# A recurrence of 1024 steps with its side work behind each step: one reciprocal, attention's product and the injections of gi, f and o each placed at another step

## The reference, cut to what matters

```python
x = x + L0(x, cond)   # attention over two keys (a learned one and one from cond), 16 heads, projected
x = x + L1(x, cond)   # mixture of experts: a shared one (silu gate) and the best 2 of 8, weighed
x = x + L2(cond, x)   # u @ W_u + x @ W_e, u from cond
x = x + L3(x, cond)   # LSTM over the 1024 positions, h0 = cond, c0 = 0

# L1: s = sigmoid(x @ router + t_bias); top 2 of s + bias; gates = s_sel / (sum(s_sel) + EPS)
#     out = (shared + sum over the two of gate * expert(x)) / 3
# L3: z = x_t @ Wx + b + h @ Wh; i, f, o = sigmoid; g = tanh; c = f * c + i * g; h = o * tanh(c)
```

## Time and profile before

| | us |
|---|---|
| median of 3 runs | 2413.18 (2410.02 to 2414.47) |
| the profiled execution: time | 2409.16 |
| its span, first to last instruction | 2407.4 |
| TensorE busy (matmul) | 2051.9 (85%) |
| VectorE busy | 1420.3 (59%) |
| POOL busy | 1169.1 (49%) |
| ScalarE busy | 876.7 (36%) |

### The profile page before, as it was taken

One profiled execution on the slowest core, in us unless ns is written; L12 is line 12 of the kernel. 1 busy time (PEld: TensorE's weight loads), 2 busy tenths in 40 slices (PEclk: granted clock), 3 DMA queues, 4 the chain that ended last, 5 costly groups with the idle time before them and its releaser, 6 DMA issues.

```text
span 2407.4 us, 200920 instructions
## 1 busy us (share of the span) xinstructions
PE 2051.9 (85%) x86306; PEld 1505.9 (63%) x86306; DVE 1420.3 (59%) x7602; ACT 876.7 (36%) x4761; POOL 1169.1 (49%) x5082
## 2 busy tenths in 40 slices
PE   6888888888888888888888888888888888888888
PEld 4666666666666666666666666666666666666666
DVE  2565665566566556656655665665566566556655
ACT  1333333333333333333333333333333333333333
POOL 3445445444544554454455445445544544544454
PEclk8999999999999999999999999999999999999999
DMA  3000000000000000000000000000000000000000
GB/s 135 4 3 2 3 3 2 2 3 3 2 3 3 2 2 3 3 2 3 3 2 2 3 3 2 3 3 2 2 3 3 2 3 3 2 2 3 3 2 3
DMA packets 57581, 14.54 MB, mean 6 GB/s; under 512 B 56161, under 2 KB 56161, under 8 KB 57058
## 3 DMA queue, kind: packets, MB, share of 16 engines
q1 hardware_dynamic: 57570, 14.39, 2.6%
HBM read 12.26 MB, written 2.10 MB: 6 GB/s over the span
## 4 chain that ended last, share of the span: by engine, by line
PE 37%; POOL 22%; DVE 20%; issue 12%; ACT 9%; DVEq 0%; POOLq 0%; ACTq 0%
PE bank L885 28%; DVE bank L678 9%; ACT terms L513 5%; DVE bank L686 5%; PE bank L792 5%; DVE h_ring L702 4%; ACT bank L519 4%; PE bank L742 3%; POOL beats L386 2%; POOL ties L387 2%; POOL ties L389 2%; POOL beats L391 2%; POOL lead L384 2%; POOL beats L358 1%; POOL top L394 1%
## 5 line engine op out<-in xcount | busy, mean ns | idle before, releaser
L885 PEld LDWEIGHTS bank<-wh_sb,h_ring 128*4 128x4 f32 (+2 forms) x65536 | 922.9, 94 | 705.9 <-DVE h_ring L702 700.1
L885 PE MATMUL bank<-wh_sb,h_ring 128*4 128x64 f32 (+2 forms) x65536 | 1107.9, 219 | 296.8 <-DVE h_ring L702 229.7
L510 ACT ACTIVATE f_act<-bank 128x4 f32<-128x4 f32 x1024 | 177.3, 173 | 1026.0 <-DVE bank L676 1026.0
L676 DVE STREAM_TRANSPOSE bank<-bank 128x64 f32<-128x64 f32 x1024 | 271.6, 265 | 390.7 <-PE bank L885 390.7
L678 DVE STREAM_TRANSPOSE bank<-bank 128x64 f32<-128x64 f32 x1024 | 271.5, 265 | 186.1 <-PE bank L885 186.1
L513 ACT ACTIVATE terms<-bank 128x8 f32<-128x8 f32 x1024 | 189.5, 185 | 280.3 <-DVE bank L678 280.3
L372 POOL TENSOR_TENSOR num<-one,fall 128x8 f32<-128x8 f32 x130 | 26.0, 200 | 532.1 <-ACT fall L467 532.1
L754 PE MATMUL bank<-up_sb,x 128*32 128x512 f32 x2080 | 274.0, 599 | 0.7 <-ACT fall L467 0.7
L684 DVE STREAM_TRANSPOSE bank<-bank 128x64 f32<-128x64 f32 x1024 | 271.6, 265 | 0.1
L760 PE MATMUL bank<-down_e,hid_t 128*16 128x256 f32 x3096 | 266.6, 380 | 0.0
L702 DVE SCALAR_TENSOR_TENSOR h_ring<-o_act,bank 128x4 f32<-128x4 f32 x1024 | 161.0, 157 | 138.6 <-ACT bank L519 95.0
(11 more groups left out here) (133 smaller groups left out, 2654.2 us busy)
## 6 DMA issues: line engine op xcount, KB each, us to landing
x_a<-in_x SPq DMA_DIRECT2D x129, 16.0 KB, 1.7
x_s<-in_x SPq DMA_DIRECT2D x129, 16.0 KB, 1.7
up_sb<-in_up SPq DMA_DIRECT2D x1, 2048.0 KB, 8.7
out_y<-y_sb SPq DMA_DIRECT2D x128, 16.0 KB, 1.4
down_sb<-in_down SPq DMA_DIRECT2D x1, 1536.0 KB, 12.5
wx_sb<-in_wx SPq DMA_DIRECT2D x1, 1024.0 KB, 14.2
wh_sb<-in_wh SPq DMA_DIRECT2D x1, 1024.0 KB, 16.3
wkv_sb<-in_wkv SPq DMA_DIRECT2D x1, 512.0 KB, 3.9
```

Source lines behind the costliest of these rows:

```text
L510: nc.scalar.activation(f_act[:, :].rearrange("p (c b) -> p c b", b=B), t_f_b[:, :, fo:fo + B], ACT.Tanh).then_inc(a_f, 1)
L676: nc.vector.transpose(bank[3][:, 0:HC], z_f_b[:, 0:HC]).then_inc(t_f, 1)
L885: last = nc.tensor.matmul(z[32 * j:32 * j + row + B, 0:HC], h_ring[:, prev, c, WIN - B - row:WIN], wh_v[:, c, g, j, :], start=False, stop= ...
```

## The change

- VectorE: `invert_inv` goes from step 5 (between scan and L702) to step 7, behind `hidden_s` and in front of the first transpose. The transpose of `hid_s` goes from the front of step 0 to step 7, between scan and L702.
- TensorE: `attend` goes from step 7 to step 3, behind `sum_mm`, and its product from bank 5 to bank 7; `x3_made` is signalled behind it. gi is injected behind step 6 (`GI_AT`), f and o behind step 7. `stream_made`, for which `attended` waits, is signalled behind `down_mm(0)` and not behind the two products of the stream.
- ScalarE and `recur`: the offsets of the rows change places between gi and f, o.
- POOL: `pad` goes from behind `gates` into it, between `lead` and `beats`, and copies other columns of x3.
- In front of the loop: a third product of attention stands behind x3, and the transpose of hid_s for the first batch of the loop is made there.

```diff
-FO_AT = 6
+GI_AT = 6
...
-        attn_b = bank[5][:, 64:64 + C * NB].rearrange("p (c t) -> p c t", c=C)
         partial_b = bank[7][:, 0:D]
         x3_b = bank[7][:, D:D + C * NB].rearrange("p (c t) -> p c t", c=C)
+        attn_b = bank[7][:, D + C * NB:D + 2 * C * NB].rearrange("p (c t) -> p c t", c=C)
+        attn_first_b = bank[6][:, C * NB:2 * C * NB].rearrange("p (c t) -> p c t", c=C)
...
+            BEHIND = (GI_AT + 1) * B
+
             def pad(count):
                 pool.wait_ge(x3_out, count)
-                return pool.tensor_copy(padded[:, :, NB:2 * NB], x3[:, :, NB:2 * NB])
+                return pool.tensor_copy(padded[:, :, NB:2 * NB], x3[:, :, BEHIND:BEHIND + NB])
...
                 pool.tensor_tensor(lead[:, :, :], rivals, own_sel, ALU.subtract).then_inc(gate_step, 1)
+                if between:
+                    between()
                 pool.wait_ge(gate_step, 7)
...
-                gates(i * U + (READY + U))
-                pad(i * U + (READY + U)).then_inc(padded_out, U)
+                gates(i * U + (READY + U), lambda: pad(i * U + (READY + U)).then_inc(padded_out, U))
                 weigh(i * U + (READY + U)).then_inc(hid_e_out, U)
...
-                    if u == 0:
-                        dve.wait_ge(hid_s_out, now)
-                        turn(0, hid_s[:, :], hid_st, U)
-                    elif u == 1:
+                    if u == 1:
...
                     elif u == 7:
-                        hidden_s(now, U)
+                        hidden_s(now)
+                        invert_inv(now)
                     dve.wait_ge(z_f, now)
...
-                    elif u == 5:
-                        invert_inv(now)
                     elif u == 6:
                         hidden_a(now)
+                    elif u == 7:
+                        dve.wait_ge(hid_s_out, now)
+                        turn(0, hid_s[:, :], hid_st, U)
...
-            pe.wait_ge(own_first, 3)
-            pe.wait_ge(hid_s_out, 3 * U)
-            attend()
...
-            sum_mm(READY)
+            sum_mm().then_inc(x3_made, READY)
+            pe.wait_ge(own_first, 3)
+            pe.wait_ge(x3_out, READY)
+            attend(attn_b)
...
-                    fo = (u + U - FO_AT - 1) % U * B
+                    gi = (u + U - GI_AT - 1) % U * B
                     now = pe.snap(t + (u + 1))
                     pe.wait_ge(hid, now)
-                    recur(z_f_b, GF, fo, prev).then_inc(z_f, 1)
-                    recur(z_gi_b, GC, u * B, prev)
-                    recur(z_gi_b, GI, 16 + u * B, prev).then_inc(z_gi, 1)
-                    recur(z_o_b, GO, fo, prev).then_inc(z_o, 1)
+                    recur(z_f_b, GF, u * B, prev).then_inc(z_f, 1)
+                    recur(z_gi_b, GC, gi, prev)
+                    recur(z_gi_b, GI, 16 + gi, prev).then_inc(z_gi, 1)
+                    recur(z_o_b, GO, u * B, prev).then_inc(z_o, 1)
                     if u == 0:
 
                         pe.wait_ge(hid_st, now)
-                        stream_mm(U)
+                        stream_mm()
                         cond_mm()
-                        down_mm(0)
+                        down_mm(0).then_inc(stream_made, U)
...
                     elif u == 3:
                         pe.wait_ge(partial_out, now)
-                        sum_mm(U)
+                        sum_mm()
+                        pe.wait_ge(own_out, now)
+
+                        attend(attn_b).then_inc(x3_made, U)
...
                     elif u == 6:
+                        pe.wait_ge(padded_out, now)
+                        pe.wait_ge(t_gi, now)
+                        inject_gi()
+                    elif u == 7:
                         pe.wait_ge(t_f, now)
                         inject_fo(z_f_b, GF)
                         pe.wait_ge(t_o, now)
                         inject_fo(z_o_b, GO)
-                    elif u == 7:
-                        pe.wait_ge(padded_out, now)
-                        pe.wait_ge(t_gi, now)
-                        inject_gi()
-                        pe.wait_ge(own_out, now)
-                        attend()
```

More of the change, by code:

```diff
@@ L362, in add_eight, with gates @@
                 pool.tensor_tensor(out, terms[:, :, 0:1], terms[:, :, 1:2], ALU.add).then_inc(gate_step, 1)
-            def gates(count):
+            def gates(count, between=None):
                 rivals = sel[:, :].unsqueeze(1).to_broadcast([P, E, E])
@@ L585, in invert_inv, with attended @@
                 nc.vector.reciprocal(inv[:, :], den_eps[:, :]).then_inc(inv_out, U)
-            def attended(src):
-                nc.vector.tensor_tensor(x1[:, :, :, 0:NB], attn_b.unsqueeze(2).to_broadcast([P, C, J, NB]),
+            def attended(attn, src):
+                nc.vector.tensor_tensor(x1[:, :, :, 0:NB], attn.unsqueeze(2).to_broadcast([P, C, J, NB]),
                                         src.unsqueeze(2).to_broadcast([P, C, J, NB]), ALU.add).then_inc(x1_out, U)
@@ L594, in hidden_a, with hidden_s @@
                                                op0=ALU.add, op1=ALU.mult).then_inc(hid_a_out, U)
-            def hidden_s(count, up_to):
+            def hidden_s(count):
                 dve.wait_ge(hid_a_out, count)
-                nc.vector.tensor_tensor(hid_s[:, :], hid_a[:, :], units[:, P:2 * P], ALU.mult).then_inc(hid_s_out, up_to)
+                nc.vector.tensor_tensor(hid_s[:, :], hid_a[:, :], units[:, P:2 * P], ALU.mult).then_inc(hid_s_out, U)
             def turn(unit, src, done, up_to):
@@ L615, in _ @@
             dve.wait_ge(attn_made, 1)
-            attended(x_first[:, 0, :, :])
+            attended(attn_first_b, x_first[:, 0, :, :])
             mask_first(1)
@@ L621, in _ @@
             hidden_a(U)
-            hidden_s(U, U)
+            hidden_s(U)
             dve.wait_ge(hid_s_out, U)
@@ L632, in _ @@
             dve.wait_ge(attn_made, 2)
-            attended(x_first[:, 1, :, :])
+            attended(attn_first_b, x_first[:, 1, :, :])
             mask_first(2)
@@ L643, in _ @@
             hidden_a(2 * U)
-            hidden_s(2 * U, 2 * U)
+            hidden_s(2 * U)
             dve.wait_ge(x3_made, READY)
             layer3(READY)
+            dve.wait_ge(hid_s_out, 2 * U)
+            turn(0, hid_s[:, :], hid_st, U)
             dve.wait_ge(w_in["wh"], 16)
@@ L738, in scores, with attend @@
                     nc.tensor.matmul(scores_b, score_w[:, c, :], x_s[:, c, :], start=(c == 0), stop=(c == C - 1))
-            def attend():
+            def attend(attn):
                 for c in range(C):
-                    last = nc.tensor.matmul(attn_b[:, c, :], value_w[:, c * P:(c + 1) * P], w1_own[:, :],
+                    last = nc.tensor.matmul(attn[:, c, :], value_w[:, c * P:(c + 1) * P], w1_own[:, :],
                                             start=True, stop=True)
@@ L761, in tile_mm, with stream_mm @@
                                         skip_group_check=True)
-            def stream_mm(up_to):
+            def stream_mm():
                 for c in range(C):
                     last = tile_mm(c, x1[:, c, 0, 0:NB], we_sb[:, c, :], True)
-                last.then_inc(stream_made, up_to)
+                return last
             def cond_mm():
@@ L776, in down_mm, with sum_mm @@
                 return last
-            def sum_mm(up_to):
+            def sum_mm():
                 for c in range(C):
@@ L781, in sum_mm @@
                                             start=True, stop=True)
-                last.then_inc(x3_made, up_to)
+                return last
             wh_v = wh_sb[:, :, :].rearrange("p c (g j m) -> p c g j m", g=4, j=J)
@@ L795, in inject @@
                 return last
-            BEHIND = (FO_AT + 1) * B
             def inject_fo(z, g):
-                return inject(z, g, NB, x3[:, :, BEHIND:BEHIND + NB], ones[:, 16:32], True)
+                return inject(z, g, NB, x3[:, :, NB:2 * NB], ones[:, 16:32], True)
             def inject_gi():
@@ L821, in _ @@
             pe.wait_ge(own_first, 1)
-            attend().then_inc(attn_made, 1)
+            attend(attn_first_b).then_inc(attn_made, 1)
             pe.wait_ge(value_out, 3)
@@ L831, in _ @@
             pe.wait_ge(we_ident, C)
-            stream_mm(READY)
+            stream_mm().then_inc(stream_made, READY)
             pe.wait_ge(w_in["wproj2"], 16)
@@ L839, in _ @@
             pe.wait_ge(own_first, 2)
+            attend(attn_first_b).then_inc(attn_made, 1)
+            pe.wait_ge(x1_out, 2 * U)
             pe.wait_ge(hid_s_out, U)
-            attend().then_inc(attn_made, 1)
-            pe.wait_ge(x1_out, 2 * U)
             route()
```

11 lines of the change are left out of this document (5 added, 6 removed).

## The result

The changed kernel takes 2218.28 us (median of 4 runs, 2215.42 to 2219.01) against 2412.98 (the median of 4 as well; the 2413.18 above is that of 3): ratio 0.9192, 95% interval 0.9176 to 0.9208. The forecast was 2209 in a range of 2201 to 2247. The direction, the two places and the range hold; 9 us of the forecast gain did not come, and 2218.28 lies 1.3 over the stretch of 2201 to 2217 that the prediction gave 0.70.

What follows compares the result with a forecast made beforehand. The prediction took one ring's latency across engines as the bound, with side work delaying steps 5 and 7. It summed 129.3 + 76.2 - 1 = 204.5 us off, giving 2204.7, plus 4.0 to the median: about 2209, range 2201 to 2247.

Steps and rivals of the forecast that it cites:

- the two places: Step 5, where L702 is 1.03 us late behind the reciprocal, and step 7, where TensorE is 0.60 late.
- gi's overrun: Rival: gi's injection overruns step 6, 17 us more, 2226; chance 0.10.
- the prediction's own sign: The prediction is wrong if a step other than 0 is over 2.1; that step names the failed part.
- part 4: POOL's pad moves between lead and beats; beats and all behind come 0.3 us later, the waiting reciprocal having 1.1 slack.
- The reciprocal, 129 us: VectorE's last reciprocal leaves step 5, and the wait holding L702 goes: 1.01 x 128 = 129.3 us gained.
- Step 7 from 2.68 to 2.08: TensorE's step 7 swaps gi's injection and attention's product for the injections of f and o: 76.2 us gained.
- The bound from above: TensorE's jump at the end of step 7, taken from VectorE's 0.45: 0.16 us late, 20 us over 127 batches.
- the jump shows: Rival: TensorE's jump to the loop's head, with 0.29 us of cover, adds 20 us: 2229; chance 0.12.
- gi's injection in step 6 costs nothing: TensorE's injection of gi in step 6 ends at 1.98, before 2.08; cost taken as 0, at most 17 us.
- POOL and h_read: half_h ends by 1213.85, before L702 of step 0 at 1214.7, 0.85 spare; rival POOL bound, 2292, chance 0.04.
- The transpose in step 7, and step 0 as before: VectorE's transpose of hid_s, moved between scan and L702 in step 7, costs nothing; step 0 keeps its 2.14.
- Slower by instruction fetch: Rival: each jump at the loop's head costs the first entry's 2.28 us gap, giving 2461; chance 0.02.

Runs made afterwards that it cites:

- e2: Kernel before, with the last reciprocal moved to step 7 and pad between lead and beats, TensorE's order unchanged: 2286.8 us, ratio 0.9481.
- e1: Kernel before, with only the last reciprocal moved from step 5 to step 7 behind hidden_s: 2420.88 us, ratio 1.0040.
- e5: e4 with the injections back where they were, f and o behind step 6, gi behind step 7: 2226.1 us, ratio 0.9237.
- e4: Changed kernel, with pad on POOL later, behind the three additions of s_sum and in front of den_eps: 2206.79 us, ratio 0.9152.
- e6: Changed kernel, with one more unused 128x8 addition on POOL between pad and beats: 2207.16 us, ratio 0.9160.
- e7: e4 with VectorE's step 0 wait for h_read moved earlier, in front of the wait for a_f: 2196.95 us, ratio 0.9120.
- e8: Changed kernel, with POOL's two-input product of ties and order table replaced by a one-input product with one: 2215.07 us, ratio 0.9179.
- e3: Changed kernel, with attention's product left in step 7 in bank 5 and x3_made signalled behind sum_mm: 2259.87 us, ratio 0.9374.

## Why the prediction was right, and where it was off

The forecast places and their sizes were right; one term of 11 us is missing from the sum and from the rivals. That 2218.28 is in the range is in part luck: the room above 2217 was kept for the jump and for gi's overrun, neither of which happened, and the collision used 1.3 us of it. By the prediction's own sign, a step other than 0 over 2.1, steps 4 (2.140) and 5 (2.109) name the part that failed, and that is part 4.

1. *The reciprocal, 129 us.* Nearly right: 124.6 in e2, with pad moved; step 5 gave its 1.01, and a few hundredths of it went in other steps, the most in step 4 (0.016). The step of the prediction that took it as a gain of its own left out that pad, and so gi's injection, stands behind comb on POOL; e1 shows a loss without it.
2. *Step 7 from 2.68 to 2.08.* Right: 2.09. "The trace does not show that jump on TensorE" was wrong; the view of L890 has the branch by itself, 208 ns, and this decides against the 108 ns that the prediction quotes. The bound from above would have been 0.30 from the last load's start and not 0.45, and the changed kernel's rows give a margin of 0.06. The value taken, 0, was right, but the reason given for it was not: that L885 followed L742 without a gap before shows only that the four long loads covered the jump. The rival "the jump shows" did not happen in the changed kernel, but its mechanism is real: in e5 it costs 19 us.
3. *gi's injection in step 6 costs nothing.* Right: 2.09. Its last load ends 2.04 into the step, there and in e5, and not 1.98, so the margin is smaller than forecast. The rival of an overrun is out.
4. *pad makes beats and all behind it 0.3 later.* The shift is right: beats 0.64 into step 4 (1215.15) and not 0.39. This is the step that failed: the prediction asked who waits for POOL's later operations and found slack, and did not ask what they now start beside. They start with the scans. That is 0.06 a batch in step 4 and 0.03 in step 5, 11 us; e4 and e6 remove it in opposite ways; their spans are 2205.0 and 2204.2, where the sum below says 2202.9. The GPSIMD Engine Reference of the Trainium skill lists POOL's SBUF interfaces (section Specifications) as shared with VectorE, with contention for VectorE instructions that have two SBUF inputs, which the scan has. By that rule a collision was to be expected, and the runs agree that there is one. How much it costs, and that it does so only where the two start nearly together, is from the rows. They do not show which part of the chip the two wait for.
5. *POOL and h_read.* Right: half_h ended 1206.99, and L707 of step 0 was due near 1208.0. 1.0 was to spare, 0.85 was forecast.
6. *The transpose in step 7, and step 0 as before.* Right: 2.086 and 2.15. Why step 0 is longer than the others was left open; e7 shows it. In the mean of all batches TensorE's step 0 is 0.01 longer than before, for its scan takes 0.21, 0.05 behind the start of L434.
7. *Slower by instruction fetch.* Out: again 8 packets on the instruction queue, and the branch has the median of 208 ns in all kernels. The 2.28 us of the earlier trace rows is the first branch alone, the longest of the 129 in the view of L890.

The sum of the spans: forecast 2407.4 - 204.5 = 2202.9, measured 2216.9, 14.0 over. 18.332 - 16.833 = 1.499 a batch in place of 1.61 is 14.1 over 127 batches. The time is only 9.6 over the 2208.7, since 4 us came back because the profiled execution lies on the median this time (2218.64 against 2218.28), where that of before lay 4 below its own.

Why the changed kernel stays for dozens of batches in the one form of the collision and then in the other is not settled. A few ns in the scan's start part the two forms, and no run here varies that alone.

## What to carry to other kernels

When side work moves, look twice at each instruction that shifts: who waits for it, and beside which instruction of the critical ring it now starts. A piece moved off the path can hold a hidden chain to another wait (here pad behind the reciprocal), so find what each moved result feeds before counting the gain. In front of the engine's jump back to the loop's head, put the side work that ends earliest, and read the loop's own line for the jump's length. The term that hurt here was visible before the change, as 19 scans of 0.25 in step 6: the most of a view's least, median and most is worth a look on the critical ring.

## What the runs showed of the hardware

- An operation of POOL and a scan of VectorE with two inputs in SBUF (128x16) that start within about 0.01 us of each other: one of the two is longer. Where the scan started 1 to 3 ns behind POOL's operation, POOL's gained 0.04 (0.36, 0.42 in e8). Where it started 5 to 9 ns behind, the scan's 0.20 became 0.37 beside two inputs of 128x64 (changed kernel) and 0.28 beside one (e8).
- The further behind POOL's start the scan comes, the less it pays: 0.24 at 0.02 behind a 128x8 operation with two inputs (changed kernel), 0.21 at 0.05 behind a copy of 128x32 (changed kernel), 0.216 to 0.22 at 0.16 behind a 128x64 one (e2, e3), and nothing at 0.26 (e4) or at 0.31 (e6), though it still overlaps its end. Started 0.14 ahead of POOL's next operation, it pays nothing either (e4).
- A loop's jump on TensorE takes 0.21 us of branch, and 0.30 from the start of the last load in front to the first one behind, when no long loads cover it (e5).
- A wait for a second semaphore in front of one VectorE instruction cost 0.07 us a batch, where the wait met last stood by itself in the queue; moved three instructions up, it cost nothing that shows (e7).
